# One head pair's query blocks in front of an attention and expert kernel: a wider lead, a triangular order, warm-up matmuls, query projections moved

## The reference, cut to what matters

```python
q, k, v = (x @ Wq.T, x @ Wk.T, x @ Wv.T)            # 16 heads of 64
attn = softmax(q @ k.T / sqrt(64))                   # over all 4096 keys of the sequence
x = layernorm(x + attn @ v)
probs = softmax(x @ router_w.T + router_b)           # 16 experts, the top 6 kept
x = layernorm(x + sum_e gate[:, e] * (x @ expert_w[e]))
```

## Time and profile before

| | us |
|---|---|
| median of 3 runs | 1737.99 (1735.62 to 1738.44) |
| the profiled execution | 1736.6 |
| its span on the slowest core (core 0) | 1735.1 |
| spans of all cores | 1679.0 to 1735.1 |
| PE busy on core 0 | 1585.0 (91%) |
| ACT busy on core 0 | 1307.4 (75%) |
| DVE busy on core 0 | 728.3 (42%) |

### The profile page before, as it was taken

The page is one execution under the profiler, slowest core; times in us unless marked ns, Lnnn a source line. Parts: engine busy times, 40 slices in busy tenths (PEclk is TensorE's granted clock), DMA queues, the critical chain, the costliest instruction groups (busy, mean ns, idle before and its releaser), DMA issues.

```text
span 1735.1 us, 55148 instructions; the slowest of 8 cores (1679.0 to 1735.1 us)
## 1 busy us (share of the span) xinstructions
PE 1585.0 (91%) x23176; PEld 987.5 (57%) x23176; DVE 728.3 (42%) x1722; ACT 1307.4 (75%) x1626; POOL 72.9 (4%) x55
## 2 busy tenths in 40 slices
PE   6999999999999999999977779999959999969996
PEld 3566556555665555655645445555636666636663
DVE  3132222222222222222227777666625666636587
ACT  2799999999999999999999866565525555525453
POOL 1000000000000000000000000000000000000056
PEclk9999999999999999999998889999979999989998
DMA  9920010010100100100050041026104133104012
GB/s 148 246 58 2 2 21 2 2 21 2 20 2 2 20 2 2 21 2 2 2 99 2 2 80 20 2 51 117 33 1 99 23 78 68 32 1 99 3 75 122
DMA packets 9877, 68.95 MB, mean 40 GB/s; under 512 B 1232, under 2 KB 1264, under 8 KB 6544
## 3 DMA queue, kind: packets, MB, share of 16 engines
q0 software_dynamic: 5008, 48.46, 15.6%
q1 hardware_dynamic: 4608, 16.78, 2.6%
HBM read 105.11 MB, written 8.39 MB: 65 GB/s over the span
## 4 chain that ended last, share of the span: by engine, by line
PE 81%; issue 6%; DVE 6%; ACT 3%; DVEq 2%; DMA 1%; ACTq 0%; POOL 0%; another core or an unknown queue 0%; PEldq 0%; POOLq 0%
PE s_PS L657 26%; PE s_PS L332 14%; PE s_PS L360 14%; PE s_PS L230 9%; PE s_PS L670 6%; PE s_PS L254 6%; PE s_PS L645 4%; ACT s_PR L341 3%; DVEq L171 2%; DMA s_XT<-xs 1%; DVE s_X1B L455 1%; DVE s_ST L408 1%; DVE s_KV L269 0%; DVE s_ACC L396 0%; PE s_PS L630 0%
## 5 line engine op out<-in xcount | busy, mean ns | idle before, releaser
L341 ACT ACTIVATE s_PR<-s_PS 128x1024 bf16<-128x1024 f32 x1024 | 947.9, 1204 | 42.5 <-PE s_PS L332 40.0
L332 PE MATMUL s_PS<-s_KV 64*128 64x256 bf16 x4096 | 352.8, 275 | 46.3 <-ACT s_PR L341 36.9
L729 ACT ACTIVATE s_PR<-s_PS,s_GS 128x512 bf16<-128x512 f32 x256 | 175.0, 686 | 260.4 <-PE s_PS L657 149.2
L360 PEld LDWEIGHTS s_PS<-s_KV,s_PR 128*128 128x128 bf16 x8192 | 285.0, 98 | 111.3 <-issue 111.3
L360 PE MATMUL s_PS<-s_KV,s_PR 128*128 128x65 bf16 x8192 | 347.0, 195 | 0.8 <-issue 0.8
L733 DVE SCALAR_TENSOR_TENSOR s_PR<-s_PS,s_GS,s_PR 128x512 bf16<-128x512 f32 x256 | 190.8, 749 | 228.5 <-ACT s_PR L729 220.4
L332 PEld LDWEIGHTS s_PS<-s_KV 64*128 64x128 bf16 x4096 | 142.5, 94 | 242.3 <-issue 197.1
L657 PE MATMUL s_PS<-s_KV,s_WP 128*64 128x512 bf16 x2080 | 241.2, 384 | 7.5 <-DVEq L852 3.0
L657 PE MATMUL s_PS<-s_XT,s_WP 128*64 128x512 bf16 x2080 | 242.2, 386 | 5.7 <-DVEq L852 3.0
L230 PE MATMUL s_PS<-s_XT,s_WP 128*128 128x512 bf16 x768 | 209.0, 382 | 21.4 <-DMA s_XT<-xs 15.1
L242 DVE CAST s_KV<-s_PS 128x512 bf16<-128x512 f32 x96 | 66.3, 691 | 336.6 <-PE s_PS L230 307.5
(11 more groups left out here) (93 smaller groups left out, 687.8 us busy)
## 6 DMA issues: line engine op xcount, KB each, us to landing
s_XT<-ew POOLq DMA_DIRECT2D x8, 2048.0 KB, 18.0
s_KV<-ew POOLq DMA_DIRECT2D x8, 2048.0 KB, 18.4
s_XT<-xs POOLq DMA_DIRECT2D x8, 1024.0 KB, 35.8
s_ACC<-xtm SPq DMA_DIRECT2D x16, 512.0 KB, 17.8
y<-s_ACC SPq DMA_DIRECT2D x16, 512.0 KB, 2.6
s_WP<-wp POOLq DMA_DIRECT2D x7, 768.0 KB, 7.0
s_WP<-wp POOLq DMA_DIRECT2D x1, 512.0 KB, 14.2
s_WP<-wp POOLq DMA_DIRECT2D x1, 256.0 KB, 5.8
```

The source lines that it names most:

```text
L332: return t.matmul(PS[:, o:o + 256], kt_buf(c)[rows, (kc + k) * 128:(kc + k + 1) * 128], q_buf(c)[rows, qb * 256:(qb + 1) * 256], start=Tru ...
L341: act[n] = S.tick(lambda s: s.activation(PR[:, (n % RING) * 1024:(n % RING + 1) * 1024], PS[:, i * 1024:(i + 1) * 1024], AF.Exp, bias=-3.0 ...
L360: return t.matmul(PS[:, o:o + 65], PR[:, p:p + 128], v_buf(c)[:, v0:v0 + 65], start=(kc + k == 0 and h == 0 and q == 0), stop=(kc + k == N ...
L729: hi_tok[(u, jh)] = S.tick(lambda s, h=h, b=b: s.activation(hi(u)[:, h], bank(b), AF.Copy, bias=0.0, scale=GS[:, u % 4:u % 4 + 1]))
```

## The change

It sets `LEAD` to 4. The order of the lead becomes triangular: two query blocks start with section 0, the other two join at section 1 and catch up on its keys and those of section 0, and from section 2 on all four take their two windows of each section. The fourth block has no accumulator bank of its own: three of its four groups of columns lie behind those of block 0 in bank 6, the fourth behind those of block 1 in bank 4; its first matmul doesn't start a new accumulation. The epilogues of the four lead blocks are all issued after the last value matmul of the lead, in the order 0, 3, 1, 2.

Twenty matmuls of 512 columns on a zeroed piece of `PR` are put ahead of the first projection. The weights of Q and V of pair 0 are loaded by two transfers with a semaphore each, in place of one. In the lead, `fill` advances by 8 pieces in the first two steps only and by 4 from then on. `proj_units(c)` is now the list that is put up in pair c: Q of the pair's own sections 1 to 3 (for c > 0), K and V of the next pair, and the next pair's Q of section 0, or all four of its Q sections where the next pair is the last.

```diff
-LEAD = 3
+LEAD = 4
+WARM = 20
...
         if s == 0:
-            load(G, WP[:, 1024:3072], d_wp[0][:, 1024:3072], gW[0])
-            w_tok[(0, 1)] = w_tok[(0, 2)] = (gW[0], 16)
+            load(G, WP[:, 1024:2048], d_wp[0][:, 1024:2048], gQ)
+            w_tok[(0, 1)] = (gQ, 16)
+            load(G, WP[:, 2048:3072], d_wp[0][:, 2048:3072], gW[0])
+            w_tok[(0, 2)] = (gW[0], 16)
...
+    T.wait(V.tick(lambda v: v.memset(PR[:, 0:512], 0.0)))
+    for _ in range(WARM):
+        T.do(lambda t: t.matmul(PS[:, 0:512], PR[:, 0:128], PR[:, 0:512], start=True, stop=True))
...
-    order = [(0, qb, 4 * s + 2 * k) for s in range(NSEC) for qb in range(LEAD) for k in range(2)]
+    order = []
+    for s in range(NSEC):
+        order += [(0, qb, 4 * s + 2 * k) for qb in range(min(2 * s, LEAD)) for k in range(2)]
+        order += [(0, qb, kc) for kc in range(0, 4 * s + 4, 2) for qb in range(2 * s, min(2 * s + 2, LEAD))]
...
+    def acc_col(c, qb, g):
+
+        if leads(c, qb) and qb == 3:
+            return 6 * 512 + (4 + g) * VW if g < 3 else 4 * 512 + 4 * VW
+        return acc_bank(c, qb) * 512 + g * VW
...
-        if kc == 0:
-            claim(ab)
+        first = kc == 0 and not (leads(c, qb) and qb == 3)
+        if first:
+            claim(acc_bank(c, qb))
...
                     if kc + k == NKC - 1 and h == 1 and q == 1:
-                        epilogue(c, qb, T.tick(mm))
+                        done = T.tick(mm)
+                        if not leads(c, qb):
+                            epilogue(c, qb, done)
+                        elif qb == LEAD - 1:
+                            for qb_ in (0, 3, 1, 2):
+                                epilogue(c, qb_, done)
...
+        for g0, g1 in ((0, 3), (3, 4)) if leads(c, qb) and qb == 3 else ((0, 4),):
+            o0 = acc_col(c, qb, g0)
+            src = PS[:, o0:o0 + (g1 - g0) * VW].rearrange("p (g w) -> p g w", w=VW)
+            tok = V.tick(lambda v, g0=g0, g1=g1, src=src: v.tensor_copy(
+                ob4[:, g0:g1, 0:65], src[:, :, 0:65]))
+            free[o0 // 512] = [tok]
...
     def proj_units(c):
-        return [u for s in range(NSEC) for u in
-                ([unit_kq(c, s, 0), unit_v(c, s)] + ([unit_kq(c, s, 1)] if s < NQB // 2 else []))]
+        own = [unit_kq(c, s, 1) for s in range(1, NQS)] if c else []
+        return (own + [u for s in range(NSEC) for u in (unit_kq(c + 1, s, 0), unit_v(c + 1, s))]
+                + [unit_kq(c + 1, s, 1) for s in range(NQS if c + 1 == NPAIR - 1 else 1)])
...
         if n == NLEAD:
-            pending.extend(proj_units(1))
+            pending.extend(proj_units(0))
         if r == 4 and 0 < c < NPAIR - 1:
-            pending.extend(proj_units(c + 1))
+            pending.extend(proj_units(c))
...
-        fill(8 if n < NLEAD else 4 if c == 0 else 3)
+        fill(8 if n < 4 else 4 if c == 0 else 3)
```

More of the change, by code:

```diff
@@ L154, in build @@
     gK = mksem("gK")
+    gQ = mksem("gQ")
     gX = [mksem(f"gX{s}") for s in range(NSEC)]
@@ L315, in slot_of, with leads @@
         return n % 2 if n < NLEAD + 2 else (n - NLEAD - 2) % 3
+    def leads(c, qb):
+        return c == 0 and qb < LEAD
+    def acc_col(c, qb, g):
+        if leads(c, qb) and qb == 3:
+            return 6 * 512 + (4 + g) * VW if g < 3 else 4 * 512 + 4 * VW
+        return acc_bank(c, qb) * 512 + g * VW
     def acc_bank(c, qb):
-        return (6, 4, 5)[qb] if c == 0 and qb < LEAD else 6
+        return (6, 4, 5, 6)[qb] if leads(c, qb) else 6
     def scores(n):
@@ L349, in values @@
         T.wait(need(v_tok, (c, kc // 4)))
-        ab = acc_bank(c, qb)
-        if kc == 0:
-            claim(ab)
+        first = kc == 0 and not (leads(c, qb) and qb == 3)
+        if first:
+            claim(acc_bank(c, qb))
         for k in range(2):
@@ L356, in mm @@
                     def mm(t, h=h, q=q, k=k):
-                        o = ab * 512 + (h * 2 + q) * VW
+                        o = acc_col(c, qb, h * 2 + q)
                         p = (n % RING) * 1024 + h * 512 + k * 256 + q * 128
@@ L361, in mm @@
                                         v_buf(c)[:, v0:v0 + 65],
-                                        start=(kc + k == 0 and h == 0 and q == 0),
+                                        start=(first and k == 0 and h == 0 and q == 0),
                                         stop=(kc + k == NKC - 1), skip_group_check=True)
                     if kc + k == NKC - 1 and h == 1 and q == 1:
-                        epilogue(c, qb, T.tick(mm))
+                        done = T.tick(mm)
[4 more added lines that the diff above has]
+                                epilogue(c, qb_, done)
                     else:
@@ L374, in epilogue @@
         V.wait(done)
[L375 to L379, removed]
+        ob4 = ob.rearrange("p (g w) -> p g w", w=VW)
+        for g0, g1 in ((0, 3), (3, 4)) if leads(c, qb) and qb == 3 else ((0, 4),):
[4 more added lines that the diff above has]
+            free[o0 // 512] = [tok]
         epi_tok[(c, qb)] = tok
@@ L885, in normal2 @@
         load(Y, d_y[t * 128:(t + 1) * 128, :], acc(t), yO)
+    NQS = NQB // 2
     def proj_units(c):
-        return [u for s in range(NSEC) for u in
-                ([unit_kq(c, s, 0), unit_v(c, s)] + ([unit_kq(c, s, 1)] if s < NQB // 2 else []))]
+        own = [unit_kq(c, s, 1) for s in range(1, NQS)] if c else []
+        return (own + [u for s in range(NSEC) for u in (unit_kq(c + 1, s, 0), unit_v(c + 1, s))]
+                + [unit_kq(c + 1, s, 1) for s in range(NQS if c + 1 == NPAIR - 1 else 1)])
     per_pair = NQB * WPB
@@ L938, in build @@
         if r == per_pair // 2 and c + 2 < NPAIR:
-            assert (c, NSEC - 1) in v_tok and (c, NQB // 2 - 1) in q_tok
+            assert (c, NSEC - 1) in v_tok and (c, NQS - 1) in q_tok
             load_w(c + 2, (T.sem, T.n))
```

## The result

The changed kernel takes 1.0056 times the time of the kernel before (95% interval 1.0035 to 1.0077), which is about 1748 us on 1738.2 (the kernel before, now of four runs and not of three). That is 0.56% slower: outside the range of 1731 to 1745 us, and on the side that I had given 26%. Of its four runs two had a disturbed die and are left out; the two others took 1750.4 and 1744.7 us.

A forecast was written before the change was run, and what follows sets the result against it. TensorE was taken to bound pair 0, the exponentials pairs 1 to 6. Terms -17.3 + 6.8 + 1.9 + 3.9 + 5.6 + 0.5 = +1.4 us, laid on the median 1737.99, gave 1739.4 us; range 1731 to 1745.

The forecast's parts named there:

- The lead: Pair 0 with four lead blocks: its matmuls end at 156.2 us against 173.47, all sixty remaining steps half-filled: -17.3 us.
- The start: Warm-up and split weights before section 1: no gain, one chance in four of a lower clock; +0.5 us, bounds 0 and +2.5.
- Four epilogues: End of the lead: PE stands 6.06 us for DVE's four copies, then 0.7 us for a cast; +6.8 us together.
- The clock behind it: After the wait at the four epilogues, PE runs at the lower clock: between 0 and 2.9 us, taken as +1.9.
- Q(1,0): Start of pair 1: its Q unit of section 0, last in the list, runs at one go on the path; +3.9 us.
- The drain: Last step of pair 6: leftover 2 + 8 + 8 matmuls run before pair 7's scores, delaying its exponentials; +5.6 us.
- Sum: Whole kernel: all terms together come to +1.4 us, 1739.4 us on the median.
- lead steps over 2.1 us: Sign of being wrong: steps in the lead of over 2.1 us.
- pair 1 starting after 173 us: Sign of being wrong: pair 1 starts after 173 us, where some 165 us was forecast.
- Rival (c): Slowest core: lower clock lasts 5.7 us after the epilogues and at section 1's K, returns at Q(1,0); 1743.9 us, chance 0.23.

The follow-up runs named there:

- The experiment: Changed kernel with last-section blocks in the order 0, 3, 1, 2, accumulators of 0, 3 and 1 copied out early, rest of the epilogues spread over later steps: 1.0009.

## Why the prediction was wrong, point by point

- **The lead (-17.3 us).** This is the step that failed. "Sixty steps are left in pair 0, all half-filled" took the price of a half-filled step from rows that stand behind the lead, where three score slots turn, for 28 steps that run with two. On core 0 these 28 steps took 63.5 us (35.34 to 98.85) in place of 56.5: +7.0. Of this, 1.85 us are the gaps in which PE lacked instructions, and the rest is 0.18 us a step. The wait for the slot is nearly all of that: in the old kernel with two slots it makes 0.17 us in each step between two ends of blocks (0.13 over all 32 steps). I should have bounded the price; I took it as known.
- **The start (+0.5).** K of section 1 fell to the lower clock in the profiled run: 3.36 us in place of 1.89, and the third step began at 29.96 and not at 28.57 us, +1.4. By 35.34 us, where I had 33.6, it was +1.7. That is within the bound of +2.5, but the chance of one in four was too small (27 of 56 cores), and its cause isn't the zeros alone. That the zeros would give nothing was right, and for the reason given: the clock was down again at 11.5 to 14.7 us on all eight cores.
- **Four epilogues (+6.8).** Right in place and size: 5.87 us of gap against 6.06, and 6.2 us taken back when the gap was taken away.
- **The clock behind it (+1.9).** Right: 0.50 for the 6.75 us shown, on all eight cores alike, and 1.7 us more won by number 128 without the stall. It fell within the gap (core 0: at 105.9 us, with PE idle up to 108.91). The experiment took gap and clock away together, so the 1.7 us is not the clock's alone for certain.
- **Q(1,0) (+3.9).** Right: ACT idle 3.94 us.
- **The drain (+5.6).** Right: 5.56 us of ACT, 6.0 us between numbers 894 and 896, and shown by itself. Nothing of it is absorbed.
- **Sum.** +1.4 us became +9.0 at the last exponential (mean over the cores). The difference is 7.6 us. On core 0 the lead's steps (+7.0) and the start (+1.2 beyond its 0.5) are 8.2, and the stall with its clock came some 0.8 us cheaper than forecast (7.9 against 8.7). After that the tail of the slowest core ran 4.5 us longer in the profiled execution than before (723.4 against 718.9 us from the last exponential), but 0.7 us on the mean over the cores, so most of it is of that core and execution.

The trace of before could have warned me. Its lead steps with a whole unit (2.9 us) have no wait for a slot, but those with nothing to fill show it, at no cost there, since ACT is the bound:

```profile
77.84 0.39 PE L332 MATMUL s_PS<-s_KV 64*128 64x256 bf16 x4
78.75 0.40 PE L332 MATMUL s_PS<-s_KV 64*128 64x256 bf16 x4 [0.51 <-ACT s_PR L341]
```

And the step with the first fill of the earlier trace rows, which is half-filled and still has two slots, took 2.70 us (88.84 to 91.54), since it came with that wait.

Of the signs that the prediction had named for being wrong, two came: lead steps over 2.1 us, and pair 1 starting after 173 us (177.22). Rival (c) had the right sign, and not the mechanism: the clock cost no more than forecast behind the stall, and behind Q(1,0) it didn't fall on any core. No rival had a lead step bound by its slots.

## What to carry to other kernels

Before a step's price is carried to another place, list which buffers turn there. The same instructions with two slots instead of three took about 0.17 us more per step here, some 5 of the 17.3 us that the wider lead was to win. A longer row of work in front can lose at its end what it wins: look at what all the blocks release at one time (four epilogues, 5.87 us), what the next stage now lacks (one unit, 3.9 us), and where the list no longer fits (18 matmuls, 5.6 us).

## What I had not expected of the hardware

PE loses about 0.1 us at each change into or out of the score matmuls (64*128 in the rows), and nothing between value and projection matmuls (both 128*128): the same 28 matmuls of a step with half a K unit take 2.00 us with two such changes and 2.22 with four. And PE can lack its own instructions for 0.2 to 1.7 us while the transfers are busy: such gaps stand on every core of the changed kernel, some 256 instructions or a multiple of that apart, each ending 1.0 to 1.6 us after a 16 KB transfer of the instruction queue has landed (17 of 19). In the kernel before, at a like load, there are none of this kind.
